# One GpSimd addition ahead of every second indirect transfer instead of every one, in the first retention stage

## The chip, the cores and the metric

The kernel runs on one core of one Trainium2 chip. The metric is the device time of one launch in microseconds (us), the median of several runs. The engines of the core are TensorE (PE in the profile, its weight loads PEld), VectorE (DVE), ScalarE (ACT), GpSimd (POOL) and SyncE (SP), each with its own instruction queue; they meet through semaphores. Sixteen DMA engines move the data.

## The reference

A two-layer language model tower on 128 sequences of 128 tokens, width 128, all in float32. What it computes, in order:

```
h = tok(x)                        # three gathered rows of an 8000-row table per token, summed (conv of width 3)
h = h + retention(layernorm(h))   # 8 heads, rotary q and k, group norm of k, silu(q), scores * decay, values, + x, relu
h = h + moe(layernorm(h))         # softmax gate over 8 experts, top 2, each relu(x @ w1 + b1) @ w2 + b2
h = h + complex_retention(layernorm(h))
h = h + merged_mlp(layernorm(h))  # weights merged per sequence from 8 task vectors
```

The change lies in the first two lines: the token lookup and the first retention stage, which also sorts the tokens by expert for the third line.

## The kernel before, in words

The program has four stages after one another, each a block of five instruction streams: `retention_phase`, `experts_phase`, `complex_retention_phase` and `merged_phase`. Between two stages all engines meet.

The first retention stage handles the 128 sequences in 32 groups of four (`NG` = 32, `GB` = 4). It is a software pipeline of steps: in step s the engines work on several groups at once, each engine on its own list of pieces in a written order. GpSimd gathers the table rows of group s+3 and then scatters the rows of group s-2; TensorE adds the shifted table rows of group s+2 (`tok`, L390 and L391), VectorE finishes that sum (`h_sum`, L742), and so on down to `place_tokens` (L894), in which VectorE writes for group s-2 the places that each token's row goes to (`pos_cur`). Steps run from -4 to 34; steps 6 to 27 are a hardware loop of two steps per turn, the others are written out.

What sets the order around the change:

- `gather` (L324) issues four indirect DMAs, one per sequence of the group. Each reads 128 table rows of 1536 bytes, by the ids in `cur_ids`, into `rows` (two buffers, by the parity of the group). It first waits until the sum of the group before the last was made (`h_ready`), and `take_ids` copies the ids of the next group on GpSimd (L321). TensorE's `tok` waits for `gathered`, which counts the landing of these transfers.
- `scatter` (L339) issues eight indirect DMAs for a group: two experts for each of four sequences. Each writes 128 normalised rows of 520 bytes from `xn_mid` to the list of the chosen expert, in the DRAM tensor `sent`. It waits for `placed`, the semaphore of `place_tokens`. ScalarE (L626) waits for `scattered` before it writes the `xn_mid` of the group after the next, and the stage ends only when all scatters have landed, since the experts stage reads `sent`.
- `space_out` (L350) stands ahead of each indirect DMA, of both kinds: one GpSimd addition of a 128x128 block to itself, in a part of `tv` that no one reads in this stage (L353). It waits for the addition before it by a counting semaphore, `pool_step` for scatters and `ids_step` for gathers, which also counts the copy of `take_ids`.

So in a full step GpSimd runs twelve additions, twelve indirect DMAs and one copy. The experts stage has additions of the same kind (L1202), 192 wide, ahead of its own indirect DMAs; those are not touched.

Of the kernel before, what the change touches and what calls it, by code (L numbers as in the profile page):

```python
# [18 lines left out]
GB = 4  # L19
GT = GB * T  # L20
NG = NB // GB
# [69 lines left out]
def run_steps(eng, step, stop, first=FIRST, loop=LOOP, last=LAST):  # L91


    for n in range(first, loop):
        step(Step(n, n % 2, n // 2))
    with eng.Fori(0, (stop - loop) // 2) as j:
        step(Step(j * 2 + loop, 0, j + loop // 2))
        step(Step(j * 2 + loop + 1, 1, j + loop // 2))
    for n in range(stop, last):
        step(Step(n, n % 2, n // 2))  # L100
# [21 lines left out]
def retention_phase(nc, h_all, w_all, routing, sent_d, ids_d, table_d, wq_d, wqs_d, wkkv_d,  # L122
# [13 lines left out]
    with ExitStack() as ctx:  # L136
# [3 lines left out]
        def sem(name):  # L140
            return ctx.enter_context(nc.semaphore("a_" + name))
# [91 lines left out]
        pool_step = sem("pool_step")  # L233
        loaded = sem("loaded")
        consts = sem("consts")
        ids_step = sem("ids_step")
# [62 lines left out]
        @block.sync  # L299
        def _(sp):  # L300
            sp.dma_start(ids[:, 0:NB], ids_d).then_inc(ids_loaded, 16)
            sp.dma_start(tabs_c[:], tabs_c_d).then_inc(loaded, 16)
            sp.dma_start(tabs[:], tabs_d).then_inc(loaded, 16)
            sp.dma_start(wkkv[:], wkkv_d).then_inc(loaded, 16)
            sp.dma_start(wq[:], wq_d).then_inc(loaded, 16)
            sp.dma_start(wqs[:], wqs_d).then_inc(loaded, 16)
            sp.dma_start(gn_w[:], gn_w_d).then_inc(loaded, 16)
            sp.dma_start(gn_b[:], gn_b_d).then_inc(loaded, 16)
            sp.dma_start(gate_w[:], gate_w_d).then_inc(loaded, 16)
            sp.dma_start(gate_c[:], gate_c_d).then_inc(loaded, 16)  # L310
            sp.dma_start(slot_c[:], slot_c_d).then_inc(loaded, 16)
            sp.dma_start(tags[:], tags_d).then_inc(loaded, 16)
            sp.dma_start(routing[2][:], tabs_c_d[:, 2 * P:3 * P]).then_inc(loaded, 16)

        @block.gpsimd
        def _(pool):
            def take_ids(g):

                if g.is_past(2):
                    pool.wait_ge(gathered[g.par], g.turn * (16 * GB))  # L320
                pool.tensor_copy(cur_ids[:, g.par * GB:(g.par + 1) * GB],  # L321
                                 ids[:, bass.ds(g.n * GB, GB)]).then_inc(ids_step, 1)

            def gather(g):  # L324

                p = g.par
                pool.wait_ge(ids_step, g.n * (GB + 1) + 1)
                if g.is_past(2):
                    pool.wait_ge(h_ready, g.n - 1)
                take_ids(g.after())  # L330
                for b in range(GB):
                    space_out(spare[:, 1, :], ids_step, g.n * (GB + 1) + (b + 2))
                    pool.indirect_dma_start(  # L333
                        out=rows[:, p, b, :], out_offset=None, in_=table_d,
                        in_offset=bass.IndirectOffsetOnAxis(ap=cur_ids[:, p * GB + b:p * GB + b + 1], axis=0),
                    ).then_inc(gathered[p], 16)

            def scatter(g, parts):

                for i in parts:  # L340
                    b, k = divmod(i, 2)
                    if i == 0:
                        pool.wait_ge(placed, g.n + 1)
                    space_out(spare[:, 0, :], pool_step, g.n * (2 * GB) + (i + 2))
                    pool.indirect_dma_start(  # L345
                        out=sent_d, out_offset=bass.IndirectOffsetOnAxis(
                            ap=pos_cur[:, g.par, b, k:k + 1], axis=0),
                        in_=xn_mid[:, g.par, b, :], in_offset=None).then_inc(scattered[g.par], 16)

            def space_out(x, step, n):  # L350

                pool.wait_ge(step, n)
                pool.tensor_tensor(x, x, x, ALU.add).then_inc(step, 1)  # L353

            def step(s):
                if g := s.at(3):
                    gather(g)
                if g := s.at(-2):
                    scatter(g, range(2 * GB))

            pool.memset(ids[:, NB:], 0).then_inc(pool_step, 1)
            pool.memset(spare, 0.0).then_inc(pool_step, 1)
            pool.wait_ge(ids_loaded, 16)
            pool.wait_ge(pool_step, 2)
            take_ids(Group(0, 0, 0))
            run_steps(pool, step, NG - 4)
            for i in range(2):
                pool.wait_ge(scattered[i], (NG // 2) * (2 * GB) * 16)
            pool.wait_ge(pool_step, NG * (2 * GB) + 2)
            pool.wait_ge(ids_step, NG * (GB + 1) + 1)  # L370

        @block.tensor
        def _(pe):
# [2646 lines left out]
```

## Time and profile before

| | |
|---|---|
| Time, median of 3 runs | 2166.8 us (2163.96 to 2176.13) |
| The profiled execution's own time | 2167.65 us |
| Its span in the trace | 2165.9 us |
| First retention stage | from 0 to some 732 us |
| Experts | some 732 to 1250 us |
| Complex retention, merged MLP | the rest |
| GpSimd busy over the span | 1242.7 us (57%) |
| L345 scatters, 256 | 264.2 us, 1032 ns each |
| L333 gathers, 128 | 127.3 us, 995 ns each |
| L353 additions, 384 | 184.1 us, 479 ns each |

Busy shares over the whole span mix stages with different limits, so the stage is looked at by itself. A row of the view of instructions in order of time gives start, duration, engine, line, operation, and in square brackets how long the engine sat idle just before and what ended that. "issue" as a releaser means that the engine waited for nothing that the trace shows. An indirect DMA's row on POOL is the time in which GpSimd works on its issue; the data move afterwards.

### The profile page before, as it was taken

To read this page: it belongs to the slowest core of one execution; us is meant where nothing else is said; L and a number is where in the kernel's file an instruction comes from. 1 tells how busy PE (TensorE), PEld (TensorE's weight loads), DVE (VectorE), ACT (ScalarE), POOL (GpSimd) and SP (SyncE) were. 2 spreads that over 40 slices of the span, in tenths; PEclk is the share of its full clock that TensorE was granted. 3 is DMA by queue.
4 is the path that set the end of the run, shared out by engine and by line. 5 is a ranking of instruction groups with operands and counts; after the bars stand their busy time and mean duration, and the time that the engine had idled before them with its cause. 6 is when DMAs were issued, how large, how long until landed. Compare 5 with 4: busy or idle time off the path is not lost. (4 is left out here: it accounts for less than half of the span.)

```text
span 2165.9 us, 58044 instructions
## 1 busy us (share of the span) xinstructions
PE 1961.8 (91%) x19420; PEld 1463.7 (68%) x19420; DVE 1521.3 (70%) x4436; ACT 1339.7 (62%) x2844; POOL 1242.7 (57%) x1563
## 2 busy tenths in 40 slices
PE   5888888888888599999999959999999699999997
PEld 2555555555555377777777736777777599999997
DVE  4978888888887333333333359999998688888877
ACT  3756566665655222222222249999899598998885
POOL 5488888888876788878887821112112033333334
PEclk9999999999998699999999969999999899999999
DMA  3112122121210365555555523111110011111111
GB/s 100 40 58 69 60 65 64 60 66 57 67 55 30 113 169 160 164 162 163 164 163 161 149 78 133 40 39 39 39 45 14 15 36 40 41 41 41 41 41 35
DMA packets 113820, 168.89 MB, mean 78 GB/s; under 512 B 19234, under 2 KB 66747, under 8 KB 113572
## 3 DMA queue, kind: packets, MB, share of 16 engines
q1 hardware_dynamic: 87940, 105.22, 17.5%
q0 software_dynamic: 25760, 62.09, 9.1%
q8 instruction: 73, 1.20, 0.2%
q14 instruction: 47, 0.39, 0.1%
HBM read 121.92 MB, written 45.32 MB: 77 GB/s over the span
## 5 line engine op out<-in xcount | busy, mean ns | idle before, releaser
L1259 ACT ACTIVATE b_hT<-b_hbank,b_w 128x512 f32<-128x512 f32 (+1 forms) x156 | 98.2, 630 | 320.0 <-PE b_hbank L1229 256.3
L1203 POOL DMA_INDIRECT done<-b_y,b_row x270 | 263.6, 976 | 48.5 <-issue 44.0
L345 POOL DMA_INDIRECT sent<-a_xn_mid,a_pos_cur x256 | 264.2, 1032 | 42.3 <-issue 41.3
L1285 DVE TENSOR_SCALAR b_hT<-b_hbank,b_w 128x512 f32<-128x512 f32 (+1 forms) x156 | 105.7, 677 | 228.5 <-PE b_hbank L1229 203.4
L1239 PE MATMUL b_bank<-b_w,b_hT 128*128 128x128 f32 x2160 | 254.2, 275 | 1.0 <-DVE b_hT L1285 1.0
L1239 PEld LDWEIGHTS b_bank<-b_w,b_hT 128*128 128x128 f32 x2160 | 247.5, 192 | 1.2 <-DVE b_hT L1285 1.2
L1229 PE MATMUL b_hbank<-b_xT,b_w 128*128 128x512 f32 (+1 forms) x624 | 247.1, 539 | 0.8 <-ACT b_xT L1266 0.8
L1492 POOL TENSOR_TENSOR c_k_early<-c_xn,c_k_decay 64x512 f32<-64x512 f32 x32 | 40.7, 1273 | 340.3 <-ACT c_xn L1699 340.3
L353 POOL TENSOR_TENSOR tv<-tv 128x128 f32<-128x128 f32 x384 | 184.1, 479 | 61.8 <-DVE a_pos_cur L894 50.3
L1229 PEld LDWEIGHTS b_hbank<-b_xT,b_w 128*128 128x128 f32 x624 | 113.4, 192 | 87.5 <-issue 83.1
L1202 POOL TENSOR_TENSOR b_spacer<-b_fill 128x192 f32<-128x192 f32 x270 | 139.9, 518 | 47.9 <-DVE b_y L1293 40.0
L1857 DVE TENSOR_TENSOR c_masked<-c_bank,c_decay 128x512 f32<-128x512 f32 x256 | 162.6, 677 | 4.8 <-PE c_bank L1586 4.2
L2552 ACT ACTIVATE d_wm<-d_bank 128x448 f32<-128x448 f32 (+1 forms) x160 | 147.9, 1102 | 26.1 <-PE d_bank L2278 25.9
L2188 POOL TENSOR_TENSOR d_res<-d_res,d_b_all 128x512 f32<-128x512 f32 x32 | 40.6, 1269 | 208.8 <-ACT d_res L2571 208.8
L2731 DVE COPY d_wm<-d_bank 128x448 f32<-128x448 f32 (+1 forms) x160 | 144.6, 1054 | 21.1 <-PE d_bank L2278 21.0
L735 DVE TENSOR_TENSOR a_masked<-a_scores,a_tabs 128x1024 f32<-128x1024 f32 x128 | 152.9, 1215 | 5.4 <-issue 3.1
L2278 PE MATMUL d_bank<-d_g_diag,tv 64*128 64x112 f32 (+1 forms) x2368 | 145.2, 278 | 7.2 <-ACT d_wm L2552 5.1
L2278 PEld LDWEIGHTS d_bank<-d_g_diag,tv 64*128 64x128 f32 x2368 | 138.4, 191 | 13.0 <-ACT d_wm L2552 6.6
L333 POOL DMA_INDIRECT a_rows<-table_dram,a_cur_ids x128 | 127.3, 995 | 20.6 <-issue 20.1
L2303 PE MATMUL d_bank<-d_wm,d_hT 128*128 128x128 f32 x1024 | 135.3, 277 | 0.3
L2287 PE MATMUL d_bank<-d_xT,d_wm 128*128 128x128 f32 x1024 | 135.4, 277 | 0.0
L2287 PEld LDWEIGHTS d_bank<-d_xT,d_wm 128*128 128x128 f32 x1024 | 124.7, 192 | 8.4 <-issue 6.7
(247 smaller groups left out, 4575.7 us busy)
## 6 DMA issues: line engine op xcount, KB each, us to landing
b_w<-pack_dram SPq DMA_DIRECT2D x78, 258.0 KB
b_w<-pack_dram SPq DMA_DIRECT2D x78, 256.0 KB
c_rows<-done SPq DMA_DIRECT2D x32, 512.0 KB, 3.8
b_x<-sent SPq DMA_DIRECT2D x57, 260.0 KB
d_b_all<-b_rows SPq DMA_DIRECT2D x32, 256.0 KB, 3.4
out_dram<-h_all SPq DMA_DIRECT2D x32, 256.0 KB, 2.3
b_b<-pack_dram SPq DMA_DIRECT2D x78, 64.5 KB
tv<-tv_dram SPq DMA_DIRECT2D x1, 4736.0 KB, 16.2
```

Of the source, the lines that this page charges most:

```text
L345: pool.indirect_dma_start(out=sent_d, out_offset=bass.IndirectOffsetOnAxis(ap=pos_cur[:, g.par, b, k:k + 1], axis=0), in_=xn_mid[:, g.par, ...
L353: pool.tensor_tensor(x, x, x, ALU.add).then_inc(step, 1)
L735: v.tensor_tensor(masked[:, p, 2 * i:2 * i + 2, :, :, :].rearrange("p r b a t -> p (r b a) t"), score_banks[i][:].rearrange("p r (x t) -> ...
L1202: pool.tensor_tensor(spacer[:], blank, blank, ALU.add).then_inc(spaced, 1)
L1203: pool.indirect_dma_start(out=done_d, out_offset=bass.IndirectOffsetOnAxis(ap=row[:, s.k, j:j + 1], axis=0), in_=y[:, s.par, j, :], in_off ...
L1229: nc.tensor.matmul(h_bank[c][:, 0:s.rows], w[:, s.par, c * P:(c + 1) * P], xT[:, 0:s.rows], start=True, stop=True).then_inc(h_full, 1)
L1239: m = nc.tensor.matmul(y_bank[s.par][:, j * D:(j + 1) * D], hT[:, c, j * P:(j + 1) * P], w[:, s.par, W2 + c * D:W2 + (c + 1) * D], start=( ...
L1857: v.tensor_tensor(masked[:, p, r, :, :, :, :].rearrange("p i c k t -> p (i c k) t"), score_bank[r][:].rearrange("p (x t) -> p x t", t=L), ...
L2278: m = nc.tensor.matmul(banks[who][:, at:at + n], tv[half, blocks[j], :], g_diag[half, 0:cols[j], :], start=True, stop=True)
L2287: m = nc.tensor.matmul(banks[who][:, j * T:(j + 1) * T], wm[:, s, 0, c * P:(c + 1) * P], xT[:, q.par, s, :], start=True, stop=True)
L2552: nc.scalar.activation(wm[:, :, half, at:at + n].rearrange("p s f -> p f s"), bank[:, 0:n * SEQS].rearrange("p (f s) -> p f s", s=SEQS), A ...
L2731: v.tensor_copy(wm[:, :, half, at:at + n].rearrange("p s f -> p f s"), bank[:, 0:n * SEQS].rearrange("p (f s) -> p f s", s=SEQS)).then_inc ...
```

## The change

Every second addition is taken out, in gathers and in scatters alike, and the semaphore counts are adapted. Nothing else differs: the same twelve indirect DMAs per step, in the same order, with the same waits for other engines. In the changed kernel the lines move by one to two: the gather's DMA is L334, the scatter's L347, the addition L355.

```
@@ gather
-                pool.wait_ge(ids_step, g.n * (GB + 1) + 1)
+                pool.wait_ge(ids_step, g.n * (GB // 2 + 1) + 1)
...
                 for b in range(GB):
-                    space_out(spare[:, 1, :], ids_step, g.n * (GB + 1) + (b + 2))
+                    if b % 2 == 0:
+                        space_out(spare[:, 1, :], ids_step, g.n * (GB // 2 + 1) + (b // 2 + 2))
                     pool.indirect_dma_start(
@@ scatter
-                    space_out(spare[:, 0, :], pool_step, g.n * (2 * GB) + (i + 2))
+                    if i % 2 == 0:
+                        space_out(spare[:, 0, :], pool_step, g.n * GB + (i // 2 + 2))
                     pool.indirect_dma_start(
@@ end of the GpSimd stream
-            pool.wait_ge(pool_step, NG * (2 * GB) + 2)
-            pool.wait_ge(ids_step, NG * (GB + 1) + 1)
+            pool.wait_ge(pool_step, NG * GB + 2)
+            pool.wait_ge(ids_step, NG * (GB // 2 + 1) + 1)
```

On GpSimd, in the hardware loop, the first two gathers of a step stood like this before (`a_rows` is the gather's target, `a_pos_cur` the places, REGISTER_ALU computes the next wait value):

```order
L321 COPY a_cur_ids<-a_ids 128x4
L352 REGISTER_ALU
L353 TENSOR_TENSOR tv<-tv 128x128 [waits a_ids_step]
L333 DMA a_rows<-table_dram,a_cur_ids 128x384
L352 REGISTER_ALU
L353 TENSOR_TENSOR tv<-tv 128x128 [waits a_ids_step]
L333 DMA a_rows<-table_dram,a_cur_ids 128x384
```

And after, from the same copy on to the first scatters (x2 are two instructions directly after one another):

```order
L321 COPY a_cur_ids<-a_ids 128x4
L354 REGISTER_ALU
L355 TENSOR_TENSOR tv<-tv 128x128 [waits a_ids_step]
L334 DMA a_rows<-table_dram,a_cur_ids 128x384 x2
L354 REGISTER_ALU
L355 TENSOR_TENSOR tv<-tv 128x128 [waits a_ids_step]
L334 DMA a_rows<-table_dram,a_cur_ids 128x384 x2
L344 REGISTER_ALU
L354 ISA [waits a_placed]
L355 TENSOR_TENSOR tv<-tv 128x128 [waits a_pool_step]
L347 DMA sent<-a_xn_mid,a_pos_cur 137216x130 x2
```

Six of the twelve indirect DMAs of a step now have another indirect DMA directly before them, with no instruction and no wait in between.

At the end of the stage, on GpSimd, the last scatters stood like this before, ahead of the experts stage's first instruction, the clearing of `b_fill`:

```order
L353 TENSOR_TENSOR tv<-tv 128x128
L345 DMA sent<-a_xn_mid,a_pos_cur 137216x130
L353 TENSOR_TENSOR tv<-tv 128x128
L345 DMA sent<-a_xn_mid,a_pos_cur 137216x130
L136 UNCONDITIONAL_BRANCH
L1180 UNCONDITIONAL_BRANCH
L1182 MEMSET b_fill 128x4160
```

After:

```order
L355 TENSOR_TENSOR tv<-tv 128x128
L347 DMA sent<-a_xn_mid,a_pos_cur 137216x130 x2
L136 UNCONDITIONAL_BRANCH
L1182 UNCONDITIONAL_BRANCH
L1184 MEMSET b_fill 128x4160
```

One addition of each pair is gone there too; the last scatter still is what stands ahead of the next stage.

## Rows read from the trace of the kernel before

**Rows 1.** The page, part 2: busy tenths of GpSimd in 40 slices of the span.
```profile
POOL 5488888888876788878887821112112033333334
```

**Rows 2.** Waits from 100 to 640 us: total, times, longest.
```profile
PE a_bank L390 <- DMA a_rows<-table_dram,a_cur_ids: 51.7, 19, 4.6
...
DVE h_all L742 <- PE a_bank L391: 42.3, 19, 5.4
...
POOL tv L353 <- DVE a_pos_cur L894: 9.7, 7, 1.6
```

**Rows 3.** Groups on GpSimd, 150 to 630 us: count, busy us, mean ns, idle before.
```profile
L345 POOL DMA_INDIRECT sent<-a_xn_mid,a_pos_cur x184 | 191.0, 1038 | 30.4 <-issue 30.4
L353 POOL TENSOR_TENSOR tv<-tv 128x128 f32<-128x128 f32 x275 | 134.6, 489 | 16.5 <-DVE a_pos_cur L894 8.2
L333 POOL DMA_INDIRECT a_rows<-table_dram,a_cur_ids x91 | 88.5, 972 | 14.5 <-issue 14.5
L321 POOL COPY a_cur_ids<-a_ids 128x4 uint32 (+1 forms) x23 | 5.1, 221 | 0.1
```

**Rows 4.** GpSimd in order of time: first scatter group, then the last gather.
```profile
85.29 0.77 POOL L353 TENSOR_TENSOR tv<-tv 128x128 f32<-128x128 f32 x1 [22.27 <-DVE a_pos_cur L894]
...
631.11 0.96 POOL L333 DMA_INDIRECT a_rows<-table_dram,a_cur_ids  x1 [0.16 <-issue]
```

**Rows 5.** From a gather's end to the next places, all engines, in order of time.
```profile
315.00 0.96 POOL L333 DMA_INDIRECT a_rows<-table_dram,a_cur_ids  x1 [0.16 <-issue]
...
318.17 1.12 PE L390 MATMUL a_bank<-a_rows,a_tabs_c 128*128 128x512 f32 x2
...
321.06 0.69 DVE L742 TENSOR_TENSOR h_all<-a_bank,a_rows 128x512 f32 x1
...
336.20 0.22 DVE L894 TENSOR_REDUCE a_pos_cur<-a_picked 128x8 uint32<-128x64 f32 x1
```

**Rows 6.** A full step of VectorE, GpSimd idle for most of it.
```profile
71.07 0.68 DVE L742 TENSOR_TENSOR h_all<-a_bank,a_rows 128x512 f32<-128x512 f32 x1
...
89.17 0.68 DVE L742 TENSOR_TENSOR h_all<-a_bank,a_rows 128x512 f32<-128x512 f32 x1
```

**Rows 7.** GpSimd in order of time: gathers issued after a pause.
```profile
56.85 0.98 POOL L333 DMA_INDIRECT a_rows<-table_dram,a_cur_ids  x1 [0.44 <-issue]
57.85 0.41 POOL L353 TENSOR_TENSOR tv<-tv 128x128 f32<-128x128 f32 x1
58.42 1.23 POOL L333 DMA_INDIRECT a_rows<-table_dram,a_cur_ids  x1 [0.16 <-issue]
```

**Rows 8.** Windows around them: busy of five engines, PEclk, DMA share, GB/s.
```profile
57.40:58.00 0.60, 0.60 (x4) 0.19 (x3) 0.54 (x2) 0.40 (x1) 0.59 (x2) 1.00 0.00 0
58.00:58.40 0.40, 0.40 (x5) 0.40 (x5) 0.39 (x1) 0.30 (x1) 0.26 (x1) 1.00 0.00 0
58.40:58.80 0.40, 0.40 (x6) 0.40 (x5) 0.40 (x2) 0.19 (x1) 0.38 (x1) 1.00 0.93 150
```

**Rows 9.** GpSimd in order of time: the longest issues.
```profile
101.42 1.97 POOL L333 DMA_INDIRECT a_rows<-table_dram,a_cur_ids  x1 [0.16 <-issue]
...
144.57 1.98 POOL L333 DMA_INDIRECT a_rows<-table_dram,a_cur_ids  x1 [0.16 <-issue]
...
710.97 1.79 POOL L345 DMA_INDIRECT sent<-a_xn_mid,a_pos_cur  x1 [0.17 <-issue]
```

**Rows 10.** GpSimd in order of time: plain DMAs, four together.
```profile
749.52 2.13 POOL L1193 DMA_DIRECT2D sent<-b_fill  x4
```

**Rows 11.** The end of the stage: GpSimd's scatters, then TensorE's first work.
```profile
704.06 0.39 POOL L353 TENSOR_TENSOR tv<-tv 128x128 f32<-128x128 f32 x1 [2.54 <-DVE a_pos_cur L894]
...
729.35 0.99 POOL L345 DMA_INDIRECT sent<-a_xn_mid,a_pos_cur  x1 [0.17 <-POOL tv L353]
...
735.78 0.47 PE L1220 MATMUL b_bank<-ident_b,b_x 128*128 128x128 f32 x1 [14.37 <-DMA b_x<-sent]
```

## The prediction, made before the changed kernel was run

> **What bounds the kernel now.** I read the slices of the page first, to see in which stage the changed instructions lie and whether GpSimd counts there: it is busy for eight tenths and more in slices 4 to 11, the first retention stage [rows 1]. So I left the page and asked for the waits of that stage. TensorE waits 51.7 us for gathered rows, VectorE 42.3 us for the sum that hangs on them, and GpSimd waits only 9.7 us, for the places of the scatter [rows 2]. The reader is to see a ring: gathers feed TensorE and VectorE, VectorE's places release the scatters, and the next gathers stand behind these scatters on GpSimd.
>
> Two lengths decide the ring's period. The first is GpSimd's own work. From 150 to 630 us there are 275 additions, twelve per step, so 22.9 steps of 20.9 us. Busy times and the idle time that nothing but the issue explains (everything except the 8.2 us of waiting for places) add up to 191.0 + 134.6 + 88.5 + 5.1 + 30.4 + 8.3 + 14.5 = 472.4 us, or 20.6 us per step [rows 3]. The second is the way around: the last gather of a step is issued by 315.96 us, TensorE starts on its rows at 318.17, VectorE at 321.06, and the next step's places are there at 336.42, when GpSimd may scatter again [rows 5]: 20.46 us. Both are about as long as the step, so neither has slack, and GpSimd is a shade ahead. From the first scatter to the end of the last gather there are 26 full steps in 546.8 us, 21.0 us each [rows 4]. What the two lengths leave unexplained, 0.3 to 0.4 us, I take as the jitter between them.
>
> A third length is the floor. Between 71.07 and 89.17 us VectorE ran a full step while GpSimd sat idle for most of it (its wait before 85.29 us was 22.27 us long): 18.1 us [rows 4, 6]. No step gets shorter than that, whatever GpSimd does.
>
> **What the change removes.** Six additions per step. One is 0.489 us and 0.03 us of idle time before it (8.3 us over 275), together 0.52. An indirect DMA and the gap before it are 221.4 / 184 = 1.20 us for a scatter and 103.0 / 91 = 1.13 for a gather, 1.18 on average [rows 3]. So a transfer costs GpSimd 1.70 us today, and twelve with the copy make the 20.6. The undisturbed spacing is a little less: an addition of 0.41, a gap of 0.16 and 0.98 [rows 7]. After the change the first of each pair keeps its 1.70 and the second costs X, from the end of the first's issue to the end of its own. A step of GpSimd is then 0.22 + 6 x 1.70 + 6 X = 10.4 + 6X. With X = 1.70 nothing changes.
>
> **What X is.** No row of the trace shows an indirect DMA directly behind another, so it has to be bounded. The lower end is the issue alone without a gap, X = 1.0, as four plain DMAs in a row take 2.13 us, 0.53 each, with nothing between them [rows 10]. Less than that I exclude, since the issue itself is 0.96 to 0.99 us long in every undisturbed row. Next comes the hand-over. The gather issued at 56.85 us was done on GpSimd at 57.83, but no byte moved until about 58.4, and then the DMA engines were 93% busy [rows 7, 8]. That is 0.6 us, as long as the addition and its gap today (0.58 us). If the next issue can't begin before the transfer before it has got going, the addition only fills a pause that stays: X = 0.6 + 1.0 = 1.6. The upper end comes from issues that were held: two gathers of 1.97 and 1.98 us and a scatter of 1.79 [rows 9], and, right on top of the transfer ahead, one of 1.23 [rows 7]. If each direct follower is held like the longest of them, X = 2.0; a held issue behind a hand-over would be 2.6.
>
> Between ends of 1.0 and 2.6 I take X = 2.0. The plain DMAs are the weaker neighbour: they take 0.53 us where an indirect takes 0.98 for as many partitions, so GpSimd does something more for the indirect one, and they read no list of indices. The rows with a held issue are of the instruction in question, in this stage. And in rows 7 the follower begins at the very moment at which the transfer ahead begins; the direct follower would begin before it, where no row of this trace shows that it comes through undelayed.
>
> The Trainium skill speaks against this choice. GPSIMD Engine Reference, section 2.1 Instruction dispatch, says that the completion of an instruction holds back only who waits on its semaphore, and that a core of GpSimd starts the next instruction as soon as it has finished its share of this one. By that rule the second of a pair starts at once and X is 1.0; the row of four plain DMAs agrees, and for indirect ones no row shows it. Perfetto Trace Analysis, section DMA Instruction — SWDGE (GPSIMD), adds that the end that a profile shows is that of writing the descriptors, not of the transfer; the pause of 0.6 us before the first byte agrees, and it does not say whether the next issue waits for it.
>
> **The sum.** With X = 2.0 a step of GpSimd is 22.4 us, longer than the way around, so the wait for places goes and the step becomes 22.4 instead of 21.0: 26 x 1.4 = +36 us. The other engines hide nothing of it, since TensorE already waits for the gathered rows and these come later. Before the first scatter and after the last gather the steps are not bound by GpSimd (22.27 us of idle time at 85.29), up to the last two groups: 16 scatters run from 704.06 to 730.34 without a break, and TensorE's first work of the next stage waits 14.37 us and starts 5.4 us behind them [rows 11]. Their eight pairs cost 8 x (2.0 - 1.64) = +3 us, by their own spacing of 26.3 / 16 = 1.64. The later stages are not touched and start behind a common meeting point, so the difference stays. From the profiled execution's own 2167.65 us (its span and 1.75 us around it) this gives 2167.65 + 39 = 2207 us; that execution is 0.9 us above the median of the runs shown, so I predict 2206.
>
> **Rivals.** (a) GpSimd goes straight on, X = 1.0. Its step is 16.4 us, below the way around. The ring then closes over two steps: places come 20.46 us after the gathers before last, then a GpSimd step follows, so two steps take 20.46 + 16.4 and one takes 18.4, just over the floor of 18.1. With 0.3 of jitter it is 18.7: 26 x (18.7 - 21.0) = -60, and 8 x (1.0 - 1.64) = -5 at the end, which makes 2103 us. It decides as soon as X falls under 1.55; with 1.3 the step is 19.6 and the time 2129. For it speak the plain DMAs [rows 10] and the floor far below today's step [rows 6]; against it, that the indirect issue is another instruction, whose length moves with what runs beside it [rows 7, 9]. It is also what the rule on dispatch would make of this kernel. (b) The pause stays and the addition was free, X from 1.6 to 1.8. GpSimd's step is 20.0 to 21.2 us; with the way around at 20.46 and the jitter the step is 20.6 to 21.2, the time 2157 to 2174. For it speaks that the pause and the addition are equally long [rows 7, 8]; against it, that nothing shows GpSimd waiting for a transfer to begin. That the change doesn't do what it says is no rival: the pairs stand directly behind one another in the order of instructions.
>
> **How the numbers follow.** A measurement of this kernel tells about 0.5% (11 us) from no change. I give X around 2.0 a chance of 0.49, (a) 0.34 and (b) 0.17. Slower by over 0.5% needs X over 1.83: 0.49. Rival (a) is faster throughout, and of (b) the lowest end, X near 1.6, would just pass the bound: faster 0.36, same 0.15. For X of 1.85 to 2.2 the likeliest case alone spans 2184 to 2241 (GpSimd's step 21.5 to 23.6). The whole range reaches down to where about half of (a) is left out, 2100, and up to 2235, with 0.05 above.
>
> **What would show it.** In the changed profile the second of each pair is to be read: its start against the end of the first, and its duration; 2.0 us together bear the forecast out, 1.0 bears out (a), 1.6 with a gap or a longer issue (b). GpSimd's wait for places should vanish if I am right and grow to 2 us per step and more in (a), where TensorE's wait for gathered rows would shrink instead. The steps between places should be 22.4 us; the last scatter should end at about 769 us, instead of 730.3. The forecast is wrong if the second issue of a pair is as short as the first with no gap, or if only some of them are held.

## The result, and the profile after the change

The changed kernel took 2221.1 us (median of 4 runs, 2217.6 to 2240.6), the kernel before 2166.5 in the same comparison: a ratio of 1.026, with a 95% interval of 1.023 to 1.029. That is 55 us slower, where 39 were forecast. The direction and the range hold. The reason does not, so the number was hit by luck, as the first view shows.

GpSimd's instructions in the changed kernel's first retention stage, 150 to 630 us (columns as in [rows 3]; lines have moved by one or two, so the gather is L334, the scatter L347, the addition L355):

```profile
L347 POOL DMA_INDIRECT sent<-a_xn_mid,a_pos_cur x168 | 172.8, 1028 | 39.4 <-issue 39.4
L334 POOL DMA_INDIRECT a_rows<-table_dram,a_cur_ids x84 | 82.1, 977 | 19.4 <-issue 19.4
L355 POOL TENSOR_TENSOR tv<-tv 128x128 f32<-128x128 f32 x125 | 61.5, 492 | 96.0 <-DVE a_pos_cur L896 92.4
L321 POOL COPY a_cur_ids<-a_ids 128x4 uint32 x21 | 4.2, 200 | 0.1
```

There are six additions per step now, so 125 of them are 20.8 steps of 23.0 us. Everything but the 92.4 us of waiting for places is 172.8 + 82.1 + 61.5 + 4.2 + 39.4 + 19.4 + 3.7 = 383.1 us, which is 18.4 us per step. GpSimd's own work fell from 20.6 us per step [rows 3] to 18.4, and 92.4 / 20.8 = 4.4 us of waiting came in its place. The forecast was 22.4 us of work and no waiting.

The waits of 100 to 640 us (who waited, for what: us in total, times, longest) say where the step's length comes from now:

```profile
POOL tv L355 <- DVE a_pos_cur L896: 104.1, 23, 8.3
PE a_bank L443 <- ACT a_kT L672: 47.0, 20, 4.6
ACT a_kT L672 <- remote: 45.6, 13, 5.1
DVE h_all L820 <- remote: 26.9, 14, 3.6
PE a_bank L392 <- DMA a_rows<-table_dram,a_cur_ids: 3.2, 1, 3.2
```

TensorE hardly waits for gathered rows any more (51.7 us in [rows 2], now 3.2). GpSimd waits for places ten times as long as before. And there is a releaser that the profile before did not have, "remote": a wait that ends where no instruction of this core has just ended. L672 (ScalarE) and L820 (VectorE) both read what TensorE wrote. Here is one such place: the last gather of the step before, then chosen rows of TensorE, ScalarE, VectorE and GpSimd from 317 to 333 us (start, us, engine, line; in brackets the idle time before):

```profile
306.69 0.94 POOL L334 DMA_INDIRECT a_rows<-table_dram,a_cur_ids  x1 [0.30 <-issue]
...
317.71 0.99 POOL L347 DMA_INDIRECT sent<-a_xn_mid,a_pos_cur  x1 [0.17 <-issue]
318.77 1.95 PE L500 MATMUL a_bank<-a_tabs_c,a_z 128*128 128x128 f32 x16
319.00 0.97 POOL L347 DMA_INDIRECT sent<-a_xn_mid,a_pos_cur  x1 [0.30 <-issue]
319.99 0.42 POOL L355 TENSOR_TENSOR tv<-tv 128x128 f32<-128x128 f32 x1
320.56 0.60 PE L453 MATMUL a_bank<-a_tabs_c,a_kn 128*128 128x128 f32 x4
320.57 0.99 POOL L347 DMA_INDIRECT sent<-a_xn_mid,a_pos_cur  x1 [0.17 <-issue]
321.29 0.91 PE L443 MATMUL a_bank<-a_wkkv,a_xT 128*128 128x384 f32 x2
321.86 1.35 POOL L347 DMA_INDIRECT sent<-a_xn_mid,a_pos_cur  x1 [0.30 <-issue]
323.74 0.78 ACT L672 ACTIVATE a_kT<-a_bank,a_gn_b,a_gn_w 128x512 f32<-128x512 f32 x1 [2.94 <-remote]
323.80 0.69 DVE L820 SCALAR_TENSOR_TENSOR h_all<-a_bank,h_all 128x512 f32 x1 [1.43 <-remote]
324.67 0.56 PE L443 MATMUL a_bank<-a_wkkv,a_xT 128*128 128x384 f32 x1 [2.47 <-ACT a_kT L672]
...
329.84 1.22 DVE L737 TENSOR_TENSOR a_masked<-a_scores,a_tabs 128x1024 f32<-128x1024 f32 x1 [0.92 <-remote]
...
332.53 0.22 DVE L896 TENSOR_REDUCE a_pos_cur<-a_picked 128x8 uint32<-128x64 f32 x1
```

TensorE's four matmuls for the keys (L453) end at 321.16, and the ScalarE instruction that waits only for them starts at 323.74. The matmuls of L500 end at 320.72, and VectorE's sum starts at 323.80. Two engines, waiting for two different results, are let go within 0.06 us of each other: it is the news that is late, not one of the results. The profile models the ends of matmuls, but the next matmul of TensorE (L443) starts at 321.29, so TensorE itself had gone on by then. The trace also holds the moment at which each semaphore was raised. From 100 to 640 us, 178 of TensorE's 535 signals were raised over 0.5 us after the end of the instruction that makes them, in bursts; in the kernel before it was 4 of 515, none of them by over 0.7 us. Signals of the other three engines were punctual in both.

The ring takes up these delays. The gathers issued by 307.63 us lead to the places that GpSimd uses from 332.92, in its second scatter group after them (the ring closes over two steps, as rival (a) says). So the way around was 332.53 + 0.22 - 307.63 = 25.1 us, against 20.46 in [rows 5]. Of these 4.7 us more, the late signal for the keys makes 2.58 and VectorE's wait for "remote" at 329.84 makes 0.92. Over the whole stage the steps were 22.5 us long: the last gather of the stage starts at 669.78, 38.7 us later than in [rows 4], spread over 26 steps. Then come the last two groups of scatters and the next stage's first matmul, the answer to [rows 11]:

```profile
753.96 0.39 POOL L355 TENSOR_TENSOR tv<-tv 128x128 f32<-128x128 f32 x1 [7.95 <-DVE a_pos_cur L896]
776.52 0.97 POOL L347 DMA_INDIRECT sent<-a_xn_mid,a_pos_cur  x1 [0.30 <-issue]
782.96 1.12 PE L1222 MATMUL b_bank<-ident_b,b_x 128*128 128x128 f32 x4 [13.87 <-DMA b_x<-sent]
```

TensorE enters the next stage at 782.96 us instead of 735.78, 47.2 us later. The whole profiled execution is 2217.6 - 2167.7 = 50 us longer. So the loss sits in the first retention stage, and the later stages keep it as it is.

### The profile page after: what moved, and what is told of

It is laid out like the page before. It is cut to its first block and busy times, and to the rows that moved or that the text cites. A ratio compares the mean times of both kernels' runs of the same rounds, so it can differ in the third digit from the quotient of the medians.

```text
span 2215.7 us, 57720 instructions
## 1 busy us (share of the span) xinstructions
PE 1994.7 (90%) x19420; PEld 1486.4 (67%) x19420; DVE 1512.3 (68%) x4436; ACT 1341.3 (61%) x2844; POOL 1149.3 (52%) x1371
## 5 line engine op out<-in xcount | busy, mean ns | idle before, releaser
L347 POOL DMA_INDIRECT sent<-a_xn_mid,a_pos_cur x256 | 262.3, 1024 | 60.0 <-issue 59.9
L443 PE MATMUL a_bank<-a_wkkv,a_xT 128*128 128x384 f32 x256 | 125.3, 576 | 80.2 <-ACT a_kT L672 53.0
L355 POOL TENSOR_TENSOR tv<-tv 128x128 f32<-128x128 f32 x192 | 95.4, 497 | 172.7 <-DVE a_pos_cur L896 167.2
L2554 ACT ACTIVATE d_wm<-d_bank 128x448 f32<-128x448 f32 (+1 forms) x160 | 146.8, 1102 | 25.5 <-PE d_bank L2280 25.1
L334 POOL DMA_INDIRECT a_rows<-table_dram,a_cur_ids x128 | 125.3, 979 | 29.6 <-issue 28.8
L443 PEld LDWEIGHTS a_bank<-a_wkkv,a_xT 128*128 128x128 f32 x256 | 42.8, 206 | 138.0 <-issue 137.1
```

The source lines that it names most:

```text
L347: pool.indirect_dma_start(out=sent_d, out_offset=bass.IndirectOffsetOnAxis(ap=pos_cur[:, g.par, b, k:k + 1], axis=0), in_=xn_mid[:, g.par, ...
L443: nc.tensor.matmul(work[K_BANK[b]][:, 0:3 * D], xT[:, g.par, b * T:(b + 1) * T], wkkv[:], start=True, stop=True).then_inc(k_full, 1)
L2554: nc.scalar.activation(wm[:, :, half, at:at + n].rearrange("p s f -> p f s"), bank[:, 0:n * SEQS].rearrange("p (f s) -> p f s", s=SEQS), A ...
```

## The experiments

After the result two things were to be told apart: what a direct follower costs GpSimd, and whether the late signals belong to the change, to the placing of the program or to the chip. The twelve runs were on four chips. Each comparison has its own runs of the kernel before, with medians of 2168 to 2171 us on these four and 2166.5 in the first comparison. Ratios within 2% of 1 are small differences, even where their interval leaves out 1. The last column is for 100 to 640 us.

| run | edit | us | ratio, 95% interval | chip | TensorE signals over 0.5 us late |
|---|---|---|---|---|---|
| (result) | the change | 2221.1 | 1.026 (1.023 to 1.029) | not known | 178 of 535 |
| e1_gather_pairs | pairs in gathers alone | 2141.5 | 0.988 (0.986 to 0.991) | 10 | none |
| e2_scatter_pairs | pairs in scatters alone | 2133.5 | 0.983 (0.981 to 0.986) | 10 | none |
| e3_two_ahead | pairs, no addition dropped | 2185.6 | 1.008 (1.005 to 1.011) | 10 | none |
| e4_narrow8 | no pairs, additions 8 wide | 2113.5 | 0.975 (0.973 to 0.977) | 10 | none |
| c1_changed_again | the change | 2187.4 | 1.008 (1.005 to 1.011) | 4 | 194 of 556 |
| c2_changed_padded | the change, program shifted | 2189.8 | 1.008 (1.005 to 1.010) | 4 | 186 of 538 |
| c3_one_per_group | one addition per group | 2297.3 | 1.061 (1.055 to 1.066) | 4 | 165 of 501 |
| c4_before_again | none | 2175.2 (one run) | - | 4 | 6 of 500 |
| d1_changed | the change | 2116.2 | 0.975 (0.972 to 0.977) | 0 | none |
| d2_scatter_pairs | as e2 | 2132.2 | 0.982 (0.980 to 0.984) | 0 | none |
| d3_narrow8 | as e4 | 2112.5 | 0.973 (0.971 to 0.975) | 0 | none |
| f1_alternating | pairs and narrow additions in turns | 2112.4 | 0.973 (0.970 to 0.976) | 2 | none |

**One half of the change at a time.** Only `if b % 2 == 0:` ahead of the gathers' addition (e1), or only `if i % 2 == 0:` ahead of the scatters' (e2).

> Pairs in the gathers alone (2 of 6 pairs of a step), scatters with an addition ahead of each. Theory T, direct follower: while an indirect DMA directly follows another on GpSimd, signals of TensorE reach the others 1 to 3 us late; each direct follower costs alike, so a third of the loss: 2166 + 55/3 = about 2185 us, ratio 1.009, and ScalarE and VectorE rows that end on 'remote' in the stretch of the gathers only. Rival R1, time between starts: the same here, 2185. Rival R2, it is the faster rhythm of GpSimd as a whole (its step is shorter, transfers bunch): a third or less, 2166 to 2185, spread over the step.

> Pairs in the scatters alone (4 of 6 pairs of a step), gathers with an addition ahead of each. T: two thirds of the loss, 2166 + 37 = about 2203 us, ratio 1.017. R1: the same, 2203. R2: about the same, 2190 to 2205. If the kind of transfer matters (writes to DRAM against reads), e1 and e2 leave the 1 to 2 proportion.

Both halves were faster, by 28 and 36 us, and no wait in either had "remote" as its releaser. All three theories had asked for 2166 to 2185 us in e1 and 2190 to 2205 in e2. Neither half of the change made anything slower on this chip, which did not fit the first result.

**Pairs with all additions kept.** e3 issues both additions of a pair ahead of it:

```diff
-                    space_out(spare[:, 0, :], pool_step, g.n * (2 * GB) + (i + 2))
+                    if i % 2 == 0:
+                        for m in range(2):
+                            space_out(spare[:, 0, :], pool_step, g.n * (2 * GB) + (i + m + 2))
```

> As many additions as before, but both of a pair stand ahead of the first transfer and none between the two. T: as many direct followers as in the change and 6 x 0.52 us more of GpSimd work a step, which stays under 21.1 us; about 2221 to 2230 us, ratio 1.025 or a little over. R1 (starts 1.29 us apart in a pair): the same. R2 (faster rhythm of GpSimd as a whole): nothing is faster on average, so 2166, ratio 1.00.

GpSimd's rows of e3, 150 to 600 us:

```profile
L349 POOL DMA_INDIRECT sent<-a_xn_mid,a_pos_cur x167 | 169.9, 1017 | 38.2 <-issue 38.2
L357 POOL TENSOR_TENSOR tv<-tv 128x128 f32<-128x128 f32 x248 | 113.2, 456 | 24.7 <-DVE a_pos_cur L898 11.4
L335 POOL DMA_INDIRECT a_rows<-table_dram,a_cur_ids x82 | 82.9, 1011 | 18.7 <-issue 16.0
```

A scatter with its gap is (169.9 + 38.2) / 167 = 1.25 us, a gather 1.24. Between two separate transfers the gap is 0.17 us, and between direct followers 0.30. With 248 / 12 = 20.7 steps in 450 us the step is 21.8 us, and nearly all of it is GpSimd's work. The additions cost time where they stand, in a place of their own, and cover nothing. Six followers cost 6 x (0.30 - 0.17) = 0.8 us per step more than separate transfers, and over 26 steps that is 20 us, where 16 were measured. So a pair by itself is a small loss; what the change can gain is the six additions that it drops. The theories on record had 2166 us or 2221 and more for this kernel, and none of them holds.

**Short additions.** e4 leaves an addition ahead of every transfer, but works on 8 columns in place of 128 (`spare[:, 0, 0:8]`).

> An addition ahead of every transfer as before, but 8 columns wide instead of 128, some 0.13 us long. The pause from one issue's end to the next start is then 0.02 + 0.13 + 0.16 = 0.31 us, as long as the 0.30 us of a direct follower in the change, but with an instruction in it. T (what counts is that the follower is direct): no late signals; GpSimd's step is 0.2 + 12 x 1.33 = 16.2 us, the ring goes to about 18.7 us and the time to about 2105, ratio 0.97. R1 (what counts is the time between starts): all twelve are now close, twice the loss of the change or so, 2220 to 2280. R2: more than the loss of the change, over 2221.

Two successive rows of GpSimd in e4:

```profile
302.25 0.20 POOL L353 TENSOR_TENSOR tv<-tv 128x8 f32<-128x8 f32 x1
302.62 0.99 POOL L345 DMA_INDIRECT sent<-a_xn_mid,a_pos_cur  x1 [0.17 <-issue]
```

The addition shrinks from 0.41 to 0.20 us, and GpSimd saves 12 x 0.21 = 2.5 us per step without one direct follower. Its medians, 2113.5 and 2112.5 us, lie 3 to 4 us under the best one of the change (2116.2).

**The change itself, on a second chip, and shifted in memory.** A first theory was that late signals came from where the changed program lies. c2 therefore replaces one memset by 16 small ones and is otherwise the change:

```diff
-            pool.memset(spare, 0.0).then_inc(pool_step, 1)
+            for i in range(16):
+                m = pool.memset(spare[:, i // 8, i % 8 * 16:i % 8 * 16 + 16], 0.0)
+            m.then_inc(pool_step, 1)
```

> The changed kernel itself, again. In its trace signals of TensorE (rows that end on 'remote') came 1 to 4 us late all through the first retention, and in none of the four kernels tried so far, though one of them has the same pairs. Theory D, the pattern: pairs of both kinds with one addition each bring this about; then again about 2221 us, ratio 1.025, and rows on 'remote'. Theory C, the chip: the late signals belong to the chip of that launch; on another chip they are gone, GpSimd's step of 17.7 us lets the ring run at 18.7 to 19.2 us, and the time is 2105 to 2120, ratio 0.975. Theory L, the layout of the program in memory: as D here, since the program is the same.

> The changed kernel, but the clearing of the additions' block at the start of GpSimd's list is cut into 16 small instructions, 15 more than before; the steps of the pipeline are the same instruction for instruction, and only their place in memory moves by 15 instructions. D: as the changed kernel, 2221, late signals. L: no late signals, 2105 to 2120. C: as c1_changed_again.

Both were 0.8% slower than the kernel before, a small loss and not the 2.5% that theory D forecast, and both had late signals. The waits for "remote" from 100 to 640 us, first c1, then c2:

```profile
ACT a_kT L672 <- remote: 38.5, 12, 3.5
DVE h_all L820 <- remote: 14.5, 10, 2.0
```

```profile
ACT a_kT L674 <- remote: 57.2, 19, 4.2
DVE h_all L822 <- remote: 20.9, 15, 2.0
```

The shifted program does as the unshifted one, so a shift by 15 instructions changes nothing; placing as such is made unlikely, and d1 below rules it out, since there the unshifted program has no late signal.

**More direct followers.** c3 keeps one addition ahead of a group's four gathers and one ahead of its eight scatters (`if b == 0:`, `if i == 0:`): ten direct followers per step in place of six, and less work for GpSimd than in any other kernel here.

> One addition ahead of the four gathers of a group and one ahead of its eight scatters, ten direct followers of twelve. GpSimd's step is 0.2 + 12 x 1.27 + 2 x 0.43 or so = 16.3 us. D: late signals, more of them than in the change, so 2221 or more. L and C: the ring runs at its floor of 18.7 us or so, 2100 to 2115, as with the narrow additions (2113.5).

> The kernel before, again, for its trace on this chip: 2166 to 2172 us. Its first trace had four signals of TensorE over 0.5 us late among 515, the four kernels tried since none. C: none here, if this is another chip than the first; D and L say nothing.

c3 was the slowest of all. Its four runs spread from 2258.6 to 2315.9 us, 4 to 7% above the kernel before, so the ratio of 1.061 is rough. Its waits, 100 to 640 us, in the trace of the 2258.6 us run:

```profile
POOL tv L355 <- DVE a_pos_cur L896: 159.4, 22, 11.5
ACT a_kT L672 <- remote: 70.1, 14, 8.4
DVE h_all L820 <- remote: 49.9, 16, 6.9
```

Single waits reach 8.4 us, where the change had 3.5 on this chip and 5.1 in the first result. The share of late signals is a third as before; they are later, not more. The kernel before, on the same chip, had 6 late signals of 500, none by over 1 us. So on this chip the delays come with fewer additions between the transfers, and they grow when more are taken out. Whether the direct followers do it or the closer rhythm of the issues isn't shown: every kernel with pairs that ran here had both. e3, which has the pairs and all additions, and e4, which has the rhythm and no pairs, ran on chip 10 alone or on chips 10 and 0.

**The change on a third chip.** d1, with e2 and e4 once more beside it:

> The changed kernel a third time, now beside two of the kernels that were fast on another chip. So far: the changed kernel has late signals of TensorE on two occasions (ratios 1.026 and 1.008), and the kernels with pairs of one kind alone and with narrow additions have none, but they ran on another chip than the second of these. Theory D, the pattern: late signals here too, ratio 1.01 to 1.03, whatever the chip. Theory C, the chip: with late signals only if the other two kernels of this call have them too; on a chip without them about 2110, ratio 0.97.

> Pairs in the scatters alone, again. Here it stands beside the changed kernel on the same chip. D with a threshold (four pairs of a step do no harm, six do): no late signals, ratio 0.983 as before, while the changed kernel has them. C: the same as the changed kernel in whether there are late signals; if there are, the time is 2166 to 2190, ratio 1.00 to 1.01.

> The additions 8 columns wide ahead of every transfer, again. If an instruction between two indirect DMAs is what keeps TensorE's signals in time (theory T), no late signals and ratio 0.975 as before, also on a chip where the changed kernel has them. If the pause matters (R1), late signals on such a chip as in the changed kernel, which has the same 0.3 us, and a ratio of 1.01 or more.

The same program that was 2.6% and 0.8% slower is now 2.5% faster. Its waits from 100 to 640 us, with no "remote" among them:

```profile
POOL tv L355 <- DVE a_pos_cur L896: 36.4, 20, 6.4
PE a_bank L392 <- DMA a_rows<-table_dram,a_cur_ids: 17.0, 20, 2.8
```

The place in d1 that answers to the one shown above, 310 to 315 us:

```profile
310.30 2.05 PE L500 MATMUL a_bank<-a_tabs_c,a_z 128*128 128x128 f32 x16 [0.73 <-ACT a_z L606]
311.85 0.99 POOL L347 DMA_INDIRECT sent<-a_xn_mid,a_pos_cur  x1 [0.17 <-issue]
312.19 0.60 PE L453 MATMUL a_bank<-a_tabs_c,a_kn 128*128 128x128 f32 x4
312.83 0.78 ACT L672 ACTIVATE a_kT<-a_bank,a_gn_b,a_gn_w 128x512 f32<-128x512 f32 x1 [0.80 <-PE a_bank L453]
313.14 1.28 POOL L347 DMA_INDIRECT sent<-a_xn_mid,a_pos_cur  x1 [0.30 <-issue]
313.49 0.69 DVE L820 SCALAR_TENSOR_TENSOR h_all<-a_bank,h_all 128x512 f32 x1
```

GpSimd does the same things in the same places. ScalarE starts 0.04 us after the last matmul for the keys, where in the first result it started 2.58 us after it. GpSimd's groups of d1, 150 to 600 us, are those of the first result too:

```profile
L347 POOL DMA_INDIRECT sent<-a_xn_mid,a_pos_cur x187 | 192.0, 1027 | 43.9 <-issue 43.9
L334 POOL DMA_INDIRECT a_rows<-table_dram,a_cur_ids x92 | 93.4, 1016 | 21.3 <-issue 21.3
L355 POOL TENSOR_TENSOR tv<-tv 128x128 f32<-128x128 f32 x139 | 66.6, 479 | 29.4 <-DVE a_pos_cur L896 25.4
```

A scatter and its gap are (192.0 + 43.9) / 187 = 1.26 us here and (172.8 + 39.4) / 168 = 1.26 there. What a direct follower costs GpSimd is the same in both. What differs is when TensorE's signals are raised.

**Pairs and narrow additions in turns.** f1 has pairs in every second step and 8-wide additions in the others. It was to show, on a chip with late signals, whether they come only while pairs run.

> Both patterns in one kernel, so that they share a chip: in even steps the pairs of the changed kernel (an addition 128 wide ahead of every second transfer), in odd steps an addition 8 wide ahead of every transfer. Whether TensorE's signals come late has so far gone with the launch: on two occasions of the changed kernel they did, on a third they didn't, and then it took 2116 us. On a chip without late signals: 2110 to 2120, ratio 0.975, nothing to be told apart but that. On a chip with them: theory T (the direct follower holds them) gives rows that end on 'remote' in even steps alone, and 2140 to 2165; R1 (the pause of 0.3 us is what counts, with an instruction in it or not) gives them in odd steps as well, and 2170 to 2220.

Its chip had none, so the question stayed open. It was as fast as e4: 0.973.

## Why the prediction was right and wrong

**What bounds the kernel: right.** The two lengths, GpSimd's work and the way around, decide the step. d1 shows it most plainly, since both can be read there between its places of 302.12 and 340.50 us:

```profile
302.12 0.68 POOL L355 TENSOR_TENSOR tv<-tv 128x128 f32<-128x128 f32 x1 [1.79 <-DVE a_pos_cur L896]
319.38 0.95 POOL L334 DMA_INDIRECT a_rows<-table_dram,a_cur_ids  x1 [0.30 <-issue]
340.50 0.68 POOL L355 TENSOR_TENSOR tv<-tv 128x128 f32<-128x128 f32 x1 [0.94 <-DVE a_pos_cur L896]
```

GpSimd works from 302.12 to 320.33, 18.2 us. The way around from there is 20.17 us. Together they are 38.4 us for two steps, 19.2 each, as rival (a) has it. With GpSimd's mean of 426.1 / 23.2 = 18.4 us (the groups of d1 above, its copies of 4.8 and 0.1, without the 25.4 of waiting) and the 20.46 of [rows 5] the rule gives 19.4 us. Over the stage the steps of d1 are (590.4 - 87.9) / 26 = 19.3 us, from its first scatter group to the end of its last gather.

**What X is: wrong, and this is the step that failed.** I took 2.0 us between bounds of 1.0 and 2.6, because held issues of up to 1.98 us were rows of the same instruction. The direct follower waits 0.30 us and takes 0.97 to 1.35. By the groups X is (18.4 - 10.4) / 6 = 1.33 us, in the first result and in d1. Of the bounds' neighbours the plain DMAs were the nearer one, and held issues like those of [rows 9] stayed the exception. The pause of 0.6 us before the first byte is no pause for GpSimd. The Trainium skill's rule (GPSIMD Engine Reference, section 2.1 Instruction dispatch), that the next instruction begins once a core has finished its share of the last, was the better guide. The traces agree with it up to the 0.30 us between two direct followers, against 0.17 behind an addition.

**The sum: its direction and its range came out by luck.** With X = 1.3 the text itself names a step of 19.6 us and 2129 us. (Its bound of 1.55, under which rival (a) decides, is too low by its own terms: GpSimd's step falls under the way around at (20.46 - 10.4) / 6 = 1.68.) d1 took 2116. So by its own terms the forecast should have been "faster", and on chip 0 it would have missed on the wrong side. In the first comparison the time was 2221 because the way around grew. 22.5 us per step and 18.4 of GpSimd's work ask for 2 x 22.5 - 18.4 = 26.6 us of way around on average, 6 more than before. TensorE's own work explains little of it: its busy time per step rose by 0.9 us with the granted clock, 0.91 where it had been 0.97. The columns of these two rows, the changed kernel of the first comparison and then d1, are the stretch, its us, busy us and instructions of TensorE, its weight loads, VectorE, ScalarE and GpSimd, granted clock, DMA share and GB/s:

```profile
200.00:600.00 400.00, 340.50 (x2326) 211.32 (x2326) 308.11 (x1028) 232.40 (x469) 267.88 (x334) 0.91 0.19 57
```

```profile
200.00:600.00 400.00, 369.16 (x2779) 227.76 (x2778) 364.95 (x1192) 275.48 (x561) 317.87 (x394) 1.00 0.23 69
```

340.5 us over 400 / 22.5 steps are 19.2 us of TensorE per step, against 17.8 in d1 and 348.08 / 19.0 = 18.3 before. e3 ran at 0.93 without a late signal, so the low clock alone does not bring the delays. What is left of the 6 us, about 5, I put down to the late signals. That is a remainder and not a measured sum, but in the place shown above 3.5 of the 4.7 us are waits for them, and the same program without them took 105 us less. No rival had them. All cases that I weighed asked what the pairs cost GpSimd, and none what they do to other engines.

**The end of the stage: the wrong sign.** I charged 3 us for the last 16 scatters. They ran from 753.96 to 777.49, 23.5 us where they had been 26.3, so 3 us were won. The 11 us that the places for them came later, with a wait of 7.95 us before them, more than took that back: 38.7 + 11.2 - 2.8 = 47.1 us, the delay seen at the next stage.

**What would show it: the signs named were of use.** A longer wait for places (it grew tenfold), TensorE's wait for rows gone, a second issue of 1.3 us: all three spoke for rival (a) in a kernel that had become slower. That contradiction led to the "remote" rows.

**What stays open.** Three chips (10, 0, 2) showed no late signal in eight kernels, six of them with pairs. Chip 4, and the first comparison's, which is not known, showed them in each kernel with direct followers. Whether that is the chip, something else that ran on it at the time, or the launch isn't shown, since each chip was used at one time only.

That GpSimd's issues bring them where they occur is borne out by the times in the four traces that have them (the first result, c1, c2 and c3, 100 to 640 us). Of some 630 signals of TensorE whose instruction ended over 0.7 us after an issue of GpSimd, none was late. During the first two issues after a pause of GpSimd of over 1 us and just behind them, 9 of 199 were; from the third issue on it was 676 of 1119. So the delay builds up within a row of issues and is gone soon after it. How it does that, and why it doesn't on the other chips, isn't shown. A narrow addition between the issues, or pairs with all additions kept, never ran on an affected chip, so what in the pattern matters stays open too.

e4 is the best version of these: 2.5 to 2.7% faster than the kernel before on chips 10 and 0, and on chip 0 level with the change (2112.5 and 2116.2 us). Whether it keeps its gain on a chip like 4 isn't shown. It has no direct followers, but its pauses between issues are nearly as short, some 0.4 us against 0.30.

## What to carry to other kernels

An instruction that seems to do nothing between two DMA issues may still keep something apart, and it can be made short before it is taken out: on chips without late signals 8-wide additions gave the gain of the change (2.5 to 2.7%) without one direct follower. When a change makes its own engine faster and the kernel slower, look among the waits for a releaser that was not there before, and compare the end of an instruction with the start of the one that waits only for it. A result of one or two per cent that hangs on issues standing close together should be repeated on another chip before it is believed, since the same program was 2.5% faster, 0.8% slower and 2.6% slower here.

## What the runs showed of the hardware

- A GpSimd indirect DMA directly behind another starts 0.30 us after the first one's issue ends; behind an addition it is 0.16 to 0.17 us. Its own length stays 0.97 us, with some of 1.26 to 1.35.
- Signals of TensorE can be raised late, up to 8.4 us as the longest wait for one (c3), and in bursts, while those of ScalarE and GpSimd in the same stretch are on time (a median of about 0.01 us). VectorE's are too, but for eight in c3 that were 0.8 to 1.6 us late. A third of TensorE's signals were over 0.5 us late in the three kernels with direct followers on chip 4 and in the first result, about one in a hundred in the kernel before, and none on chips 0, 2 and 10, in 583 to 669 signals per kernel.
- Where they occur, the late ones go with GpSimd's indirect DMA issues: none of some 630 made over 0.7 us after an issue was late, and over half of those made from the third issue of a row on.
- The kernel before hardly tells the chips apart: medians of 2168 to 2171 us on each of the four.
- An addition of 128 columns takes GpSimd 0.41 us, one of 8 columns 0.20: most of a short one is not its columns.
